# State-space phase of a two-FFN, one-Mamba block: a joint operand for the time steps' weights, an earlier product of B and C, another gate in y's banks, and the state added ahead of gating

## What is computed

```
proj = h @ in_proj_w            # h: twice normalised x; columns: gate 1024 | ssm 1024 | dt 8 | B 128 | C 128
ssm  = silu(conv4(ssm) + conv_bias)
dt   = softplus(dt_raw + dt_bias);  log_a = -exp(A_log) * dt
cum  = cumsum(log_a) within a chunk
y    = (exp(cum_i - cum_j) masked to j <= i) * (C_i . B_j) * dt_j * x_j   # within the chunk
     + exp(cum_i) * C_i . state                                           # carried in
state = exp(cum_end) * state + sum_j exp(cum_end - cum_j) * dt_j * B_j x_j
out  = x + ((y + D * ssm) * silu(gate)) @ out_proj_w
```

## Time and profile before

| | us |
|---|---|
| median of 3 runs | 2482.47 (2478.77 to 2484.05) |
| profiled execution | 2475.68 |
| its span, first to last instruction | 2473.7 |
| mean granted TensorE clock | 0.982 |
| TensorE busy | 2348.6 (95%) |
| VectorE busy | 1417.9 (57%) |
| ScalarE busy | 956.5 (39%) |
| GpSimd busy | 672.0 (27%) |

### The profile page before, as it was taken

How to read it: one execution, slowest core, us unless ns; L and a number is a source line. 1 busy time by engine, 2 the same in 40 slices (tenths; PEclk the granted TensorE clock), 3 DMA queues, 4 the chain that set the end, 5 groups by cost and what they waited for, 6 DMA issues and landing times. The chain is left out here.

```text
span 2473.7 us, 41910 instructions
## 1 busy us (share of the span) xinstructions
PE 2348.6 (95%) x16736; PEld 2069.5 (84%) x16736; DVE 1417.9 (57%) x3236; ACT 956.5 (39%) x1665; POOL 672.0 (27%) x527
## 2 busy tenths in 40 slices
PE   6999999999978999999999999995999999999995
PEld 5999998787767888888888899884999998877774
DVE  5767752222227777777777777765676763232221
ACT  4232332222235554445555555543333332332220
POOL 1244443111121222222222222220144443111121
PEclk9999999999999999999999999997999999999997
DMA  7634225787753111111111111004153413877768
GB/s 245 208 137 154 74 69 197 236 247 236 238 117 99 34 27 26 27 26 27 26 27 39 31 32 30 10 10 159 67 213 105 144 54 121 245 224 225 227 160 166
DMA packets 102754, 292.82 MB, mean 118 GB/s; under 512 B 22498, under 2 KB 22754, under 8 KB 91872
## 3 DMA queue, kind: packets, MB, share of 16 engines
q1 hardware_dynamic: 54944, 198.35, 22.9%
q0 software_dynamic: 47616, 91.79, 16.4%
HBM read 197.28 MB, written 151.80 MB: 141 GB/s over the span
## 5 line engine op out<-in xcount | busy, mean ns | idle before, releaser
L1696 DVE SCALAR_TENSOR_TENSOR m_xt<-m_ssm,m_convw,m_xt 128x256 f32<-128x256 f32 x384 | 219.9, 586 | 57.8 <-ACT m_ssm L1288 48.7
L1412 PE MATMUL m_p_ab<-m_ht_hi,m_wi_b_hi 128*128 128x256 f32 x640 | 182.0, 284 | 5.3 <-ACT m_gate L1260 5.3
L1413 PE MATMUL m_p_ab<-m_ht_lo,m_wi_b_hi 128*128 128x256 f32 x640 | 179.4, 280 | 0.0
L1414 PE MATMUL m_p_ab<-m_ht_hi,m_wi_b_lo 128*128 128x256 f32 x640 | 179.3, 280 | 0.0
L390 POOL DMA_INDIRECT slot_rows<-a_hr,a_slot_now x128 | 131.1, 1024 | 139.9 <-PE p_gate_a L615 85.7
L390 POOL DMA_INDIRECT slot_rows<-b_hr,b_slot_now x128 | 130.8, 1022 | 140.0 <-PE p_gate_b L615 85.4
L613 PE MATMUL p_gate_a<-a_hts_hi,a_w_hi 128*128 128x256 f32 x512 | 149.2, 291 | 14.9 <-ACT a_silu L511 13.3
L613 PE MATMUL p_gate_b<-b_hts_hi,b_w_hi 128*128 128x256 f32 x512 | 147.4, 288 | 1.6 <-DVE b_hts_lo L874 1.4
L613 PE MATMUL p_up_b<-b_hts_hi,b_w_hi 128*128 128x256 f32 x512 | 148.3, 290 | 0.0
L613 PE MATMUL p_up_a<-a_hts_hi,a_w_hi 128*128 128x256 f32 x512 | 148.1, 289 | 0.0
L614 PE MATMUL p_gate_a<-a_hts_lo,a_w_hi 128*128 128x256 f32 x512 | 146.4, 286 | 0.0
(11 more groups left out here) (353 smaller groups left out, 7384.3 us busy)
## 6 DMA issues: line engine op xcount, KB each, us to landing
a_ew<-in_ew SPq DMA_DIRECT2D x32, 1536.0 KB, 7.5
b_ew<-in_ew SPq DMA_DIRECT2D x32, 1536.0 KB, 7.7
after_ffn<-a_zeros POOLq DMA_DIRECT2D x6, 2048.0 KB, 9.0
out<-b_zeros POOLq DMA_DIRECT2D x6, 2048.0 KB, 9.2
slot_rows<-a_zeros POOLq DMA_DIRECT2D x1, 8336.0 KB, 41.0
a_rows<-slot_rows SPq DMA_DIRECT2D x32, 260.5 KB, 8.7
b_rows<-slot_rows SPq DMA_DIRECT2D x32, 260.5 KB, 8.7
a_xr<-in_x SPq DMA_DIRECT2D x8, 1024.0 KB, 9.7
```

The costliest lines, as they stand in the source:

```text
L1412: t.matmul(out, l_hi, r_hi_, start=first, stop=False)
L1413: t.matmul(out, l_hi, r_lo_, start=False, stop=False)
L1414: return t.matmul(out, l_lo, r_hi_, start=False, stop=last)
L1696: ins_ = v.scalar_tensor_tensor(xt[:, m, :], ssm[:, m, i:i + BM], convw[:, m, i:i + 1], xt[:, m, :], ALU.mult, ALU.add)
```

## The change

- The 8 high and the 8 low columns of dt's weights stand in one operand `w_dt` of 40 columns (high at 0 to 7, low at 32 to 39, zeros between, written once in `early` under the semaphore `gap_set`). `project_dt` multiplies it by h's high and by h's low part: 8 matmuls with 40 rows of output in place of 12 with 8 rows. The copy takes 40 rows. `to_tokens` adds the two halves while it turns them: a plain float32 matmul with the constant `picks` (ones at row i and 32 + i) in place of a transpose, and it stands ahead of B's transposes, no longer behind them.
- B by C becomes job 7 (ssm 2 job 8) and is made directly behind the sums, ahead of the out product; ScalarE copies it ahead of ssm 2. It goes to `p_y`, and so does gate 4. All other jobs outside `p_x` and `p_y` share `p_ab` in turn by their place in `RING`. y's first product of a block waits for the copy of gate 4.
- In block 0, the wait for the FFN's accumulator now stands in front of B by C, not of y.
- `add_state(n, 0)` stands ahead of `gated(n, 0)` on VectorE.

```diff
-    J_DT, J_C, J_B, J_TOK, J_CUM, J_CB = 0, 1, 2, 3, 6, 8
-    J_SSM = [4, 5, 7, 9, 10, 11, 12, 13]
+    J_DT, J_C, J_B, J_TOK, J_CUM, J_CB = 0, 1, 2, 3, 6, 7
+    J_SSM = [4, 5, 8, 9, 10, 11, 12, 13]
     J_GATE = list(range(14, 22))
+    IN_X, IN_Y = [J_GATE[2], J_GATE[3]], [J_CB, J_GATE[4]]
+    RING = [job for job in range(JOBS) if job not in IN_X + IN_Y]
...
+        w_dt = sb("w_dt", [P, KD, CR], F32R)
...
+            if first == DT0:
+                return w_dt[:, :, 0:NH], w_dt[:, :, LO_AT:CR]
...
-        ab_of = lambda job: p_x[:, job % 2, :] if job in J_GATE[2:4] else p_ab[:, job % 2, :]
+        def ab_of(job):
+            for bank, jobs in ((p_x, IN_X), (p_y, IN_Y)):
+                if job in jobs:
+                    return bank[:, jobs.index(job), :]
+            return p_ab[:, RING.index(job) % 2, :]
...
-                copy_job(n, J_DT, dtt[:, :], NH)
+                copy_job(n, J_DT, dtt[:, :], CR)
...
-                ssm_job(2)
                 wait(act, decay_ready, n * TM)
                 copy_job(n, J_CB, cb[:, :, :])
+                ssm_job(2)
...
+                    a.activation(w_dt[:, :, NH:LO_AT], ..., ACT.Copy, scale=0.0).then_inc(gap_set, 1)
...
             def ab(n, job):
-                if job in J_GATE[2:4]:
+                if job in IN_X:
                     wait(pe, out_ready, n * TM)
+                elif job in IN_Y:
+                    if n == 0:
+                        pe.wait_ge(prior.acc_ready, NS * TS)
+                    wait(pe, y_read, n * TM)
                 else:
-                    before = job - 4 if job in J_GATE[4:6] else job - 2
-                    if n * JOBS + before >= 0:
-                        pe.wait_ge(ab_free, n * JOBS + before + 1)
+                    at = RING.index(job)
+                    before = n * JOBS + RING[at - 2] - (JOBS if at < 2 else 0)
+                    if before >= 0:
+                        pe.wait_ge(ab_free, before + 1)
                 return ab_of(job)
-            def project(n, job, col, width=P):
+            def project_dt(n):
+                ...
+                out = ab(n, J_DT)[0:CR, 0:BM]
+                for k in range(KD):
+                    for part in (ht_hi, ht_lo):
+                        mm = t.matmul(out, w_dt[:, k, :], part[:, k, :], start=(k == 0 and part is ht_hi),
+                                      stop=(k == KD - 1 and part is ht_lo))
+                mm.then_inc(ab_full, 1)
...
                 for j in range(TM):
-                    t.matmul(out[:, j * P:(j + 1) * P], bt[:, j * P:(j + 1) * P], c.ident[:],
-                             is_transpose=True, start=True, stop=True)
+                    at = TM * P + j * NH
+                    t.matmul(out[:, at:at + NH], dtt[:, j * P:(j + 1) * P], c.picks[0:CR, :], start=True, stop=True)
                 for j in range(TM):
-                    at = TM * P + j * NH
-                    mm = t.matmul(out[:, at:at + NH], dtt[:, j * P:(j + 1) * P], c.ident[0:NH, 0:NH],
+                    mm = t.matmul(out[:, j * P:(j + 1) * P], bt[:, j * P:(j + 1) * P], c.ident[:],
                                   is_transpose=True, start=True, stop=True)
...
             def y_product(n, j):
-                if n == 0:
-                    pe.wait_ge(prior.acc_ready, NS * TS)
+                if j == 0:
+                    pe.wait_ge(ab_free, n * JOBS + J_GATE[4] + 1)
...
                 cumulate(n)
+                b_by_c(n)
                 if not is_(n, 0):
                     out_product(n - 1, 1)
                 ssm_part(2)
-                b_by_c(n)
                 spread(n, 0)
...
                     skip_part(n, 0)
+                    add_state(n, 0)
                     gated(n, 0)
-                    add_state(n, 0)
                     halves(n, 0)
```

More of the change, by code:

```diff
@@ L1038, in mamba @@
         sb = Region(nc, "m", c.first_byte + ROUTED_AT)
-        wi_a = sb("wi_a_hi", [P, KD, SPLIT_COL], F32R), sb("wi_a_lo", [P, KD, SPLIT_COL], F32R)
+        wi_a = sb("wi_a_hi", [P, KD, SPLIT_COL - NH], F32R), sb("wi_a_lo", [P, KD, SPLIT_COL - NH], F32R)
+        w_dt = sb("w_dt", [P, KD, CR], F32R)
         h = sb("h", [P, TM, D])
@@ L1043, in mamba @@
         early = sb.next
-        dtt = sb("dtt", [NH, BM])
+        dtt = sb("dtt", [CR, BM])
         cum_t = Region(nc, "m", early)("cum_t", [NH, BM])
@@ L1093, in wi @@
         def wi(first, n):
+            if first == DT0:
+                return w_dt[:, :, 0:NH], w_dt[:, :, LO_AT:CR]
             if first < SPLIT_COL:
-                return [part[:, :, first:first + n] for part in wi_a]
+                return [part[:, :, first - NH:first - NH + n] for part in wi_a]
             i, at = divmod(first - SPLIT_COL, 2 * P)
@@ L1368, in early @@
                     a.activation(a_neg[:], a_neg[:], ACT.Exp).then_inc(a_exp, 1)
+                    a.activation(w_dt[:, :, NH:LO_AT], c.ones[:, 0:LO_AT - NH].unsqueeze(1).to_broadcast([P, KD, LO_AT - NH]),
+                                 ACT.Copy, scale=0.0).then_inc(gap_set, 1)
                     split(0)
@@ L1427, in ab, with project @@
             def ab(n, job):
-                if job in J_GATE[2:4]:
+                if job in IN_X:
                     wait(pe, out_ready, n * TM)
-                else:
-                    before = job - 4 if job in J_GATE[4:6] else job - 2
-                    if n * JOBS + before >= 0:
-                        pe.wait_ge(ab_free, n * JOBS + before + 1)
+                elif job in IN_Y:
+                    if n == 0:
+                        pe.wait_ge(prior.acc_ready, NS * TS)
+                    wait(pe, y_read, n * TM)
+                else:
+                    at = RING.index(job)
+                    before = n * JOBS + RING[at - 2] - (JOBS if at < 2 else 0)
+                    if before >= 0:
+                        pe.wait_ge(ab_free, before + 1)
                 return ab_of(job)
-            def project(n, job, col, width=P):
+            def project_dt(n):
                 if is_(n, 0):
-                    pe.wait_ge(w_lo_done, 1 if col == DT0 else (col - NH) // (2 * P) + 2)
-                out = ab(n, job)[0:width, 0:BM]
-                hi, lo = wi(col, width)
+                    pe.wait_ge(w_lo_done, 1)
+                    pe.wait_ge(gap_set, 1)
+                out = ab(n, J_DT)[0:CR, 0:BM]
[4 more added lines that the diff above has]
+                mm.then_inc(ab_full, 1)
+            def project(n, job, col):
+                if is_(n, 0):
+                    pe.wait_ge(w_lo_done, (col - NH) // (2 * P) + 2)
+                out = ab(n, job)[:, 0:BM]
+                hi, lo = wi(col, P)
                 for k in range(KD):
@@ L1543, in head @@
                 pe.wait_ge(ht_ready, n * 2 + 2)
-                project(n, J_DT, DT0, NH)
+                project_dt(n)
                 project(n, J_C, C0)
```

2 lines of the change are left out of this document (1 added, 1 removed).

## The result

| | before | after |
|---|---|---|
| median of the runs (lowest to highest) | 2483.26 us (2478.77 to 2490.32, 6 runs) | 2512.44 us (2501.13 to 2527.95, 6 runs) |
| profiled execution, its span | 2475.7, 2473.7 | 2501.1, 2499.3 |
| mean granted clock of the profiled execution (TensorE's, as a share of full speed) | 0.982 | 0.977 |
| blocks 1 to 14, first start to last end | 791.9 us (56.55 to 56.65 each) | 818.4 us (58.02 to 59.13 each) |

A block is counted here from its first sum of log_a on TensorE to the next block's. The ratio is 1.0119, 95% interval 1.0085 to 1.0153: slower. The profiled execution of after was the lowest of its six runs and 25.4 us above that of before; the medians lie 29.2 us apart. Of the 25.4, blocks 1 to 14 hold 818.4 - 791.9 = 26.5.

The account below looks back on a forecast made before the run. TensorE, busy 56.2 of 56.5 us in a block, was taken as the bound. Blocks 1 to 14 gave +21 us, the last -1.55, block 0 -0.95: +18.5, so 2494.2 profiled, 2501 as a median, range 2467 to 2508.

Parts of the forecast that it names:

- The collision, and who wins it: GpSimd's product starts 0.04 us ahead of VectorE's `mask_cb` and holds it; TensorE stalls 2.0 us ahead of spread 1.
- Rival 1: VectorE wins the collision, GpSimd waits 0.4 us; -0.5 us a block, median 2471 us; chance 0.38.
- won case: `mask_cb` starts before GpSimd's product: -11.5 us in all, 2464.2 profiled, 2471 as a median; chance 0.38.
- No second stall of size follows: Behind spread 1, the rest of VectorE's chain slips by the same 2 us, so TensorE gets no further large wait.
- gate 7: TensorE's gate 7 waits for gate 5's copy in the new ring: +0.15 us a block, between 0 and 0.3.
- The head: At a block's head, eight dt matmuls replace twelve at 0.117 us each: -0.47 us a block.
- y's stall: TensorE's wait for `add_state` ahead of y of chunk 1 goes whole: -0.38 us a block.
- Tokens: Turning dt to tokens by float32 matmul makes four records, not two: +0.2 us a block, between 0 and +0.3.
- Rival 3: The new waits lower the clock: 15 waits at about 1.7 us each, +25 us more, 2526 us; chance 0.03.
- main case: GpSimd wins the collision: +1.5 us in each of blocks 1 to 14, median 2501 us (2493 to 2508); chance 0.52.
- The last block: +2.0 + 0.15 - 3.7 = -1.55 us; the -3.7 from y's shorter wait and recovered clock, between -2.5 and -4.2.
- Block 0: No collision, as GpSimd's products come far later; with 0.3 for a gate that waits less, -0.95 us.

Follow-up runs that it names:

- run 1: The changed kernel with `mask_cb` moved ahead of convolve 2 in VectorE's order; 2458.04 us, 0.9942 times the kernel before.
- run 5: The changed kernel plus two, three or five small ScalarE copies ahead of the exponential that GpSimd waits for; ratios to before 1.0137, 1.0129 and 0.9954.
- run 7: The kernel before with only the state ahead of gating, 2463.49 us; the changed kernel with only dt's part and the new banks, 2478.31 us.
- run 2: The changed kernel with B by C, its copy and its ring place put back behind ssm 2; 2456.86 us, 0.9938 times the kernel before.
- two copies: The changed kernel plus two small ScalarE copies ahead of the exponential that GpSimd waits for; 2506.54 us, 1.0137 times the kernel before.
- three copies: The changed kernel plus three small ScalarE copies ahead of the exponential that GpSimd waits for; 2517.57 us, 1.0129 times the kernel before.
- B by C alone: The kernel before with only the move of B by C and the banks it needs; 2540.28 us, 1.0286 times the kernel before.
- run 4: The changed kernel measured again, unaltered, beside the kernel before; 2506.68 us, 1.0133 times the kernel before.
- run 6: The changed kernel with spread 1 issued one piece of the state-space projection later; 2501.89 us, 1.0111 times the kernel before.

## Why the prediction came out as it did

It said slower for the right reason, and too little: a median of 2501 us, 17.7 above the 2483.3 of the runs, where 29.2 were measured, outside its range (2508). The step that failed is the clock behind the new waits, for which the main sum had nothing: the largest miss that the profiles show. A second wait of TensorE and the gains of block 0 and the last block were mis-sized too.

The sum had +18.5 us, so 10.7 of the 29.2 are missing from it. In the profiled execution 1.9 of these are in blocks 1 to 14 at full clock (22.9 for 21), 3.6 are lowered clock in these blocks, and 1.9 are in block 0 and the last block; the rest of the kernel gives 0.5 back. The remaining 3.7 are the distance of the median from the profiled execution: 11.3 us for after, where it was 7.6 for before. The other runs of after have mean clocks of 0.965 to 0.977, but no profile, so that part isn't taken apart. Point by point:

**The collision, and who wins it: right.** GpSimd ahead of `mask_cb` by the 0.04 us that was worked out, `mask_cb` at 2.64 us, a wait of 1.85 us for the forecast 2.0 (1.7 to 2.4), in each of blocks 1 to 15. Rival 1 had its condition right as well (the order of the two starts decides at once): runs 1 and 5 turn that order round and get the gain. It gave the won case -11.5 us; run 1 has 17.8 (2458.04 for 2475.85). The Trainium skill says of VectorE and GpSimd, on its page "SBUF — State Buffer", section "Who interferes with whom", that the order of issue decides who blocks; run 5 bears that out, with the two outcomes 0.16 us apart (0.04 ahead, 0.12 behind). The same section's VectorE with one SBUF input that goes free is shown twice: `add_state` at 1.21 us, and the differences at 2.15.

One row was misread, without effect on the outcome: in block 0 VectorE's step stood still through three GpSimd operations, not two, since the state times its decay ran from 794.12 for 2.35 us ahead of the two products of the earlier trace rows. And the blocks do not repeat within 0.01 us (56.55 to 56.65); the lead of `mask_cb` over GpSimd does (0.40 to 0.41 us in blocks 1 to 15).

**"No second stall of size follows": wrong.** This is a term of the sum that was left out. The wait of 0.61 us ahead of the last gate piece is the collision's second end. In the prediction I followed VectorE's chain into TensorE and stopped; the chain also runs into ScalarE, which waits for the differences and for the convolution ahead of its copies. ScalarE's copy of gate 5, for which gate 7 waits, starts 29.5 us into the block in after, and 27.0 in run 1. I had looked at this very place (gate 7, +0.15, between 0 and 0.3) and costed it for the 0.45 us of the move alone. It is 0 without the collision (no such wait in run 1) and 0.61 with it in block 8, 0.36 to 0.82 in the eight blocks of full clock. The collision's whole price is 2.5 us by run 1.

**The small terms.** The head: 12 matmuls took 1.80 us and 8 take 1.34, -0.46 for -0.47. y's stall: -0.38 in the sum, -0.45 in a block by run 7. Tokens: +0.2 in the sum; the four records and what lies around them cost about 0.3 and the first out product gave 0.1 back. A further 0.1 us is gained between the two spreads, in matmuls that the sum left alone; its cause is open. In all, -0.82 in a block (run 2) where the sum, gate 7 included, had -0.5. With +2.5 for +2.0 the two errors nearly cancel, which is luck: +1.5 forecast, 58.2 - 56.56 = +1.64 measured in a block of full clock. Fourteen of these are 23 us for the 21 of the sum.

**The clock: the step that failed.** The sum takes the new waits at their length alone, with nothing for the clock behind them. Rival 3 said that the new waits would lower the clock, and I gave it 0.03 with a single row against it: a wait of 1.88 us that passed unharmed. One such wait says little of fifteen. With the collision the clock fell in 6, 11, 9, 11, 7 and 11 of blocks 1 to 14 (after, again, two copies, three copies, spread later, B by C alone); in the six kernels without it, the one before included, in none of 84. It took 3.6 us of the first profile and some 12 of the second. So rival 3 had the mechanism right and the price wrong: +25 us, every wait at 1.7 us. By these two profiles it belonged in the main case, as 4 to 12 us with a chance of its own. The runs of after spread by 27 us and those of before beside them by 12; that the clock in these blocks makes the difference fits the profiles but is not shown, since before spreads by up to 21 us elsewhere (run 4).

The range was also narrower than its own terms: a stall of 2.4 and tokens of 0.3 in fifteen blocks and a last block of -2.5 add 8.7 us, which is 2510 and not 2508, and with gate 7 at the 0.3 that the text allowed it, 2512.

The Trainium skill's page "TensorE: Matmul & The Clock Gate", section "Part 1: The HAM clock gate (the "warmup" mystery)", gives 2.4 GHz as the clock of a busy engine and 1.2 GHz as that of an idle one. The stretches at 0.50 and 0.51 above are at the lower of these levels. But TensorE did not stand idle before them, it worked with one wait of 1.85 us (in run 6, with waits of 0.49 and 0.71), and why the clock fell in one block and not in the next stays open.

**The last block.** It got 0.5 us shorter, where the sum had 1.55. The shorter wait came as forecast: 1.86 us for 4.45. That the clock then stays up did not, in this execution. y of chunk 1 in after (timeline):

```profile
1700.58 0.46 PE L1544 MATMUL m_p_y<-m_decay,m_xdt 128*128 128x128 f32 x2 [1.86 <-DVE m_state L1772]
```

The window behind that start:

```profile
1700.60:1704.10 3.50, 3.50 (x21) 3.50 (x22) 2.38 (x2) 1.06 (x1) 2.93 (x2) 0.64 0.02 5
```

In run 1 the same wait (timeline):

```profile
1659.76 0.46 PE L1544 MATMUL m_p_y<-m_decay,m_xdt 128*128 128x128 f32 x2 [1.86 <-DVE m_state L1772]
```

is followed by a clock of 1.00 (windows):

```profile
1659.80:1663.30 3.50, 3.50 (x32) 3.50 (x32) 2.38 (x2) 1.06 (x1) 2.92 (x2) 1.00 0.00 0
```

Over all profiles, the wait of 1.86 us had a lowered clock behind it in two of nine; at that of 4.45 us it was lowered in three of three. Without the collision the last block falls from 60.3 to 56.1 us by the state's part alone: 4.2, the upper end of the -3.7 that I gave (-2.5 to -4.2).

**Block 0: not settled.** -0.95 was forecast and -0.02 measured. It came to 61.40 with the state's part, 61.25 with dt's, 57.88 with both, and 62.11 in run 1. Its waits for ScalarE's gate copies (4.97 us in one place before, 3.53 and 2.00 in two after) and its lowered clock differ from kernel to kernel, and no run takes them apart. It also has a small wait that the sum did not have, 0.51 us ahead of spread 1. It happens once, and the most it moves is 4 us.

## What to carry to other kernels

Before work is moved so that a chain starts earlier, look at what that chain will meet on the port that VectorE and GpSimd share: here a product that came 0.44 us earlier cost 2.5 us in every block, and swapping two calls in VectorE's order took that away. Follow a late operation down every engine that waits for it, not only to the first wait on the engine that bounds. And price a repeated new wait of TensorE with its clock: behind such waits the clock fell in 55 of 83 blocks here, and in none of 84 without them.

## What the runs showed of the hardware that I had not expected

- Where GpSimd's product (2.4 us) started 0.04 us ahead of VectorE's next operation, that operation took 2.64 us for 0.42, although its own engine handed on to it without a gap. A start 0.12 us behind costs VectorE nothing, and GpSimd's product takes 2.55 for 2.41 us.
- Delaying GpSimd's input by 0.16 us, with five copies that do nothing, took the kernel with the change from 1.0133 times the time of before (run 4) to 0.9954 times.
- The granted clock fell to its lower level in blocks whose longest wait was 0.71 us (seven of fourteen in run 6), and stayed up behind single waits of 1.86 us in seven cases of nine.
- A lowered stretch of 3.4 us cost 0.5 to 0.9 us in a block of the changed kernel and nothing in run 6; stretches of 6.8 us cost 2.0 to 2.4 us (run 4: 60.3 to 60.7 for 58.3 us).
